# Mixture-of-experts tiles: singles between the pairs, weights used in place, programs written out

## The reference

```python
# layer 0: 8 experts, hidden 1024, two of them for a token, relu
h = relu(einsum('tc,efc->tef', x, w1) + b1);  y = einsum('tef,ecf->tec', h, w2) + b2
# layer 1: 8 experts, hidden 512, two of them for a token, gated
g = silu(einsum('bsd,edh->bseh', x, w1)) * einsum('bsd,edh->bseh', x, w2)
expert_out = einsum('bseh,ehd->bsed', g, w3)
# both: the token's two rows, weighted by the router's shares, are summed
```

## Time and profile before

| | us |
|---|---|
| median of 3 runs | 1726.03 |
| lowest, highest | 1717.77, 1727.92 |
| profiled execution, in all | 1718.13 |
| its span in the profile | 1716.4 |
| TensorE busy in the span | 1490.5 (87%) |
| VectorE, ScalarE, POOL busy | 1071.8, 818.4, 698.3 |

### The profile page before, as it was taken

The page is one execution under the profiler, slowest core; times in us unless marked ns, Lnnn a source line. Parts: engine busy times, 40 slices in busy tenths (PEclk is TensorE's granted clock), DMA queues, the critical chain, the costliest instruction groups (busy, mean ns, idle before and its releaser), DMA issues. The chain is left out here.

```text
span 1716.4 us, 37753 instructions
## 1 busy us (share of the span) xinstructions
PE 1490.5 (87%) x12752; PEld 1102.5 (64%) x12752; DVE 1071.8 (62%) x1904; ACT 818.4 (48%) x1552; POOL 698.3 (41%) x495
## 2 busy tenths in 40 slices
PE   7798898897888569999999887999978589999976
PEld 2433333334227558888888775777758479999875
DVE  5687687687787834555554333888868834444433
ACT  2664755665644425555555441666745322222221
POOL 3501402204200015666665432777750046666543
PEclk8899899899895689999999997999995789999999
DMA  5411321313116465555555664100007163344475
GB/s 180 147 50 49 122 73 58 113 49 117 63 43 221 147 238 131 143 144 138 144 139 115 190 183 109 46 25 25 26 6 241 62 209 63 63 65 66 105 215 137
DMA packets 110598, 191.45 MB, mean 112 GB/s; under 512 B 10929, under 2 KB 68581, under 8 KB 110181
## 3 DMA queue, kind: packets, MB, share of 16 engines
q1 hardware_dynamic: 80407, 149.44, 26.2%
q0 software_dynamic: 27264, 37.24, 12.6%
q10 hardware_dynamic: 2791, 2.84, 0.5%
HBM read 122.53 MB, written 66.96 MB: 110 GB/s over the span
## 5 line engine op out<-in xcount | busy, mean ns | idle before, releaser
L1391 PE MATMUL e_ph<-e_zTt,weights_a 128*128 128x256 f16 x2688 | 306.1, 275 | 2.3 <-DMA weights_b<-weight_parts 1.8
L1391 PEld LDWEIGHTS e_ph<-e_zTt,weights_a 128*128 x2688 | 262.5, 98 | 40.2 <-issue 8.4
L1321 POOL DMA_INDIRECT e_zt<-token_parts,slot_token x142 | 153.1, 1078 | 208.8 <-issue 199.2
L1474 ACT ACTIVATE e_h<-e_ph,e_b 128x256 f32<-128x256 f32 (+1 forms) x344 | 128.0, 434 | 208.6 <-PE e_ph L1391 146.6
L1529 DVE TENSOR_TENSOR e_hl<-e_h,e_hh 128x512 f16<-128x512 f32 x142 | 94.3, 690 | 202.8 <-ACT e_hh L1489 202.8
L1332 POOL DMA_INDIRECT token_rows<-e_ysb,slot_token x71 | 147.0, 2071 | 175.1 <-DVE e_ysb L1558 156.6
L1407 PE MATMUL e_pyt<-weights_b,e_hh 128*128 x1136 | 194.5, 274 | 4.3 <-issue 3.1
L704 ACT ACTIVATE probs<-lower_banks,shift 128x1024 f32<-128x1024 f32 x128 | 137.3, 1112 | 90.3 <-PE lower_banks L578 88.7
L1332 POOL DMA_INDIRECT out_dram<-e_ysb,slot_token x71 | 113.0, 1591 | 126.3 <-DVE e_ysb L1562 103.0
L1407 PE MATMUL e_pyt<-weights_b,e_hl 128*128 x568 | 155.5, 274 | 0.0
L739 DVE TENSOR_TENSOR acc<-acc,probs 128x1024 f32<-128x1024 f32 (+1 forms) x112 | 136.8, 1222 | 23.2 <-ACT probs L704 19.9
(11 more groups left out here) (251 smaller groups left out, 3000.0 us busy)
## 6 DMA issues: line engine op xcount, KB each, us to landing
x_sb<-weight_parts SPq DMA_DIRECT2D x30, 1024.0 KB, 7.1
weight_parts<-w_split SPq DMA_DIRECT2D x32, 512.0 KB, 3.4
weights_a<-weight_parts SPq DMA_DIRECT2D x16, 1024.0 KB, 7.4
x_sb<-in_u SPq DMA_DIRECT2D x24, 512.0 KB, 5.0
weight_parts<-x_sb SPq DMA_DIRECT2D x24, 512.0 KB, 3.4
w_raw<-in_w1T SPq DMA_DIRECT2D x16, 512.0 KB, 4.5
w_raw<-in_w2T SPq DMA_DIRECT2D x16, 512.0 KB, 4.8
weights_b<-weight_parts SPq DMA_DIRECT2D x8, 1024.0 KB, 9.3
```

The lines of the kernel that those rows point to most:

```text
L1321: pool.indirect_dma_start(zt[:, i % 2, c, :], None, g.zrows, at).then_inc(ld[i % 2], 16)
L1391: last = pe.matmul(out[:, f, :], up_of(i, e, wp, k, per * q + f), zTs[:, s, 2 * zp + k, 0:cols * P], start=(n == 0), stop=(n == 5))
L1474: last = act.activation(place(h32[:, slot], per)[:, f, :], place(ph[:, bank], per)[:, f, :], ACT.Relu, bias=b1[:, bass.ds(e, 1), per * q + ...
```

## The change

The tiles come in another order: 14 pairs, then single, pair, single, ..., the 43rd a single again (`SINGLES_FROM` = 13; `single[i]` and lists beside it take the place of `extent`). `column[i]` and `expert_of` map a tile to its old place in the tables, so routing stays as it is. `fetch_own`, its buffer and its semaphores go: a single's up takes the weights in `weights_a` by register address as a pair's does. A single's units use PSUM banks 0 to 1 (layer 0) or 0 and 2 (layer 1) and bank 1 of the downs. The programs of ScalarE and VectorE are written out for every tile, with constant semaphore values. In layer 0 VectorE copies the tokens of i+2 before the last of tile i+1's subtractions instead of behind it. TensorE reads the expert numbers in the middle of a pair's down only, so two at each pair among the singles.

```diff
+SINGLES_FROM = 2 * PAIRS - NT
...
+    single = [i > SINGLES_FROM and (i - SINGLES_FROM) % 2 == 1 for i in range(NT)]
+    cols = [1 if one else C for one in single]
+    per = [4 if one else 2 for one in single]
...
-            def fetch_own(i):
-
-                s, b = i % 2, i + PAIRS
-                if i >= PAIRS + 2:
-                    sp.wait_ge(up_done, UB * b - UB)
-                e = expert_of(sp, i)
-                sp.dma_start(own_w[:, s], g.parts[layer][:, :, bass.ds(e, 1), 0:2 * F0].rearrange("p w o n -> p w (o n)")
-                             ).then_inc(own_ld[s], 16)
...
-                if single:
-                    pe.wait_ge(own_ld[s], 16 * ((i - PAIRS) // 2 + 1))
                 pe.wait_ge(zev, i + 1)
...
-                                last = pe.matmul(out[:, f, :], up_of(i, e, wp, k, per * q + f), zTs[:, s, 2 * zp + k, 0:cols * P],
-                                                 start=(n == 0), stop=(n == 5))
+                                last = pe.matmul(out[:, f, :], up_w(wp, e, k, per[i] * q + f),
+                                                 zTs[:, s, 2 * zp + k, 0:cols[i] * P], start=(n == 0), stop=(n == 5))
...
-                for c in range(extent(i)[1]):
-                    if c == extent(i)[1] - 1 and i + 2 < NT:
-                        e[i + 2] = expert_of(pe, i + 2)
+                for c in range(cols[i]):
+                    if c == 1:
+                        for n in range(i + 2, min(i + 4, NT)):
+                            if n not in e:
+                                e[n] = expert_of(pe, n)
                     down(i, c, e[i])
...
+            for i in range(NT):
+                e = expert_of(act, i) if layer == 0 else None
+                activate(i, 0, e)
+                for q in units(i)[1:]:
+                    activate(i, q, e)
+                    high(i, q - 1)
+                high(i, units(i)[-1])
+                if layer == 0 and 0 <= i - FIRST_PIECE < PIECES:
+                    weight_high(i - FIRST_PIECE)
...
+            for i in range(-1, NT):
                 if i + 1 < NT:
-                    hidden_and_next(i + 1, (i + 1) % 2, i + 2 < NT, False, i + 1 >= PAIRS, i + 2 >= PAIRS)
-                result(i, i % 2, i // 2, False, i >= PAIRS)
+                    if layer:
+                        for q in units(i + 1):
+                            gated(i + 1, q)
+                    else:
+                        for q in units(i + 1)[:-1]:
+                            low(i + 1, q)
+                    if 2 <= i + 2 < NT:
+                        evacuate(i + 2)
+                    for q in units(i + 1) if layer else units(i + 1)[-1:]:
+                        low(i + 1, q)
+                if i >= 0:
+                    result(i)
```

More of the change, by code:

```diff
@@ L1253, in experts, with units, hidden, parted @@
         up_w, down_w = g.up_w, g.down_w
[L1255 to L1268, removed]
-        def expert_of(eng, i):
-            return eng.value_load(g.expert[0:1, bass.ds(i, 1)], min_val=0, max_val=E - 1)
+        def expert_of(eng, i):
+            n = PAIRS + alone[i] if single[i] else i - alone[i]
+            return eng.value_load(g.expert[0:1, n:n + 1], min_val=0, max_val=E - 1)
+        def units(i):
+            return range(2 * cols[i]) if layer == 0 else range(cols[i])
+        def hidden(x, q):
+            return x[:, q % 2]
+        def parted(x, i):
+            return x.rearrange("p (f t) -> p f t", f=per[i])
+        def finished(i):
+            return blocks[i - 1] if i >= 1 else 0
         @block.sync
         def _(sp):
+            def fetch(j):
+                fetched = g.pieces[1][j % KINDS][0](j // KINDS)
+                sp.dma_start(raw[:, j % 2:j % 2 + 1, :].rearrange("p o (k n) -> p (o k) n", k=fetched.shape[1]), fetched
+                             ).then_inc(w_ld[j % 2], 16)
             if layer == 0:
@@ L1429, in _ @@
                               start=True, stop=True)
-        def steps(eng, body):
-            body(0, 0, True)
-            body(1, 1, True)
-            for first, last in ((1, SPLIT), (SPLIT, PAIRS // 2)):
-                with eng.Fori(first, last) as n:
-                    body(2 * n, 0, False)
-                    if layer == 0 and first == 1:
-                        weight_high(eng, n, 0)
-                    body(2 * n + 1, 1, False)
-                    if layer == 0 and first == 1:
-                        weight_high(eng, n, 1)
-            for i in range(PAIRS, NT):
-                body(i, i % 2, False, True)
@@ new lines, in low @@
+            def low(i, q):
+                n = len(units(i)) // cols[i] * blocks[i] + q
+                if q == 0 and finished(i):
+                    dve.wait_ge(dn_done, finished(i))
+                dve.wait_ge(hi_done, n + 1)
+                own = (slice(None), i % 2, slice(per[i] * q, per[i] * q + per[i]), slice(0, cols[i] * P))
+                dve.tensor_tensor(hl[own], parted(hidden(gt if layer else h32, n), i), hh[own], ALU.subtract
+                                  ).then_inc(lo_done, 1)
@@ L1546, in result @@
+            def result(i):
+                if layer == 0:
+                    if i == 0:
                         dve.wait_ge(w_kept[1], 16)
                     e = expert_of(dve, i)
-                if not early:
-                    dve.wait_ge(sto[s], landed(i) if single else 16 * C * half)
-                for c in range(cols):
-                    share = g.slot_weight[:, bass.ds(b + c, 1)]
-                    y = py[s if single else c]
+                if i >= 2:
+                    dve.wait_ge(sto[i % 2], landed[i - 2])
+                for c in range(cols[i]):
+                    share = g.slot_weight[:, column[i] + c:column[i] + c + 1]
+                    y = py[out_of(i, c)]
+                    dve.wait_ge(dn_done, blocks[i] + c + 1)
@@ L1579, in _ @@
[L1579 to L1589 removed]
+            evacuate(0)
```

250 lines of the change are left out of this document (89 added, 161 removed).

## The result

The changed kernel takes **1769.0 us** (median of 4 runs, 1764.1 to 1773.8) against 1723.4 us (1717.8 to 1727.9) for the kernel before, run on the same chip: a ratio of 1.0265, 95% interval 1.0233 to 1.0297. It is slower by 45.7 us; the forecast was 1762 us, in a range from 1732 to 1784. The profiled execution took 1768.9 us with a span of 1767.2.

The account below looks back on a forecast made before the run. TensorE was taken as nearly full, its layer-0 pair matmuls nearly equal to the ScalarE/VectorE chain. Terms 34.5 - 1.2 + 5.4 + 1.7 gave +40 us, 1758 or 1766 by base; predicted 1762 us, range 1732 to 1784.

Parts of the forecast that it names:

- Layer 0, pair to single, 10.1 us: From a pair's up to the single's: the token copy behind the pair's third subtraction sets 10.1 us, against 8.1 of matmuls.
- Layer 0, single to pair, 10.1 us: From a single's up to the next pair's: 4.1 of register steps, 0.45, 5.24 and 0.3 of expert loads.
- Layer 1, 6.8 and 7.8 us: Pair to single 6.8 us, single to pair 7.8 along the sequencer; stretch 211.5 against 206.1 us, +5.4.
- The first pairs, 0.1 us each from the earlier copy, -1.2 us: Layer 0's first 13 pairs gain 0.1 us each from the earlier copy, since matmuls then bound them.
- Fetches' cost given back whole: Fetches' waits and slowed gathers, within 1.8 us a layer-1 single, at most 27 us in all, are won back whole.
- The statement that a reordering can win little: TensorE is 95% and 92% busy in the two stretches, so reordering wins little unless TensorE works on too much.
- Scatters: Scatters and gathers stay off the path in both layers; phase ends cost 0.6 us in layer 0, 1.1 in layer 1.
- Rival 4: Much slower: scatters set the pace, 15.6 us against layer 1's 14.6 us turn; 1776 to 1788 us, chance 0.10.
- Writing out, 0 within 0 to 5 us: Written-out ScalarE and VectorE programs mean more instruction fetching: bounded by 0 and +5 us, taken as 0.
- Rival 1: Faster: register steps of a single's up are hidden, layer 1's stretch 182 us; total 1707 us, chance 0.12.
- Rival 3: No difference: steps cost but layer 0's chain doesn't, stretch 265 us; total 1732 us, chance 0.08.
- The sequencer's lead: How far TensorE's register steps run ahead: at most 18 matmuls by the row, 0.2 to 0.3 us at layer-1 singles' ups.

Follow-up runs that it names:

- warm: The changed kernel with 24 unused transposes of the identity ahead of the wait for the copy at each layer-0 single; 1755.6 us, one run.
- fixed: The changed kernel, but every single's up reads expert 0's weights at a fixed address instead of the chosen expert's by register; 1712.8 us.
- loads_early: The changed kernel with TensorE's two loads of expert numbers moved from the pair's down into the middle of its up; 1752.0 us.
- late_copy: The changed kernel with layer 0's copy of turned tokens back behind a tile's last subtraction; 1770.0 us, 2 runs.
- tail_fetch: The changed kernel with the old tile order (pairs, then singles) and the singles' weight fetches put back; 1720.0 us.
- three_regs: The changed kernel with three buffers instead of two for layer 0's hidden tile; 1733.4 us.
- tail_regs: The changed kernel with the old tile order in both layers, still with register addresses and no fetches; 1727.7 us.

## Why the prediction was right, step by step

- **Layer 0, pair to single, 10.1 us**: 9.99. The mechanism is shown from both sides: a third buffer makes it 8.14, a later copy 10.59.
- **Layer 0, single to pair, 10.1 us**: 10.44 to 10.54 but for the first. The sum held at the full clock (10.04 in `warm`); what failed is that it took the clock of before for granted across a new gap. The fall to 1.2 GHz stretches the up from 4.2 to 4.8 us; it also gives the sequencer time, so that the loads' gap of 0.3 us, which the sum had, is covered. With the clock held the stretch is 293.8 us against 295.4 forecast.
- **Layer 1, 6.8 and 7.8 us**: 6.77 and 7.8 to 8.1, 214.3 us against 211.5. Steps and loads are both shown, by `fixed` (5.9) and `loads_early` (7.2).
- **The first pairs, 0.1 us each from the earlier copy, -1.2 us**: right in sign, but mostly not by that cause. `late_copy` has the copy in its old place and still 10.93 us a pair; the copy gave 0.6 us of 2.3, other edits the rest.
- **Fetches' cost given back whole**: right in sign, small in size. Alternating, fetching costs 3.1 us in layer 1 and 0.5 in layer 0. What hurt before was fetches and gathers crowded into a stretch of singles (12.4 us of waits in `tail_fetch`). The statement that a reordering can win little was wrong for layer 1: it wins 17.4 us when nothing else is changed.
- **Scatters**: no wait of TensorE for them or for gathers. POOL waited for its own scatters twice in layer 0's stretch (2.2 and 5.2 us) and never in layer 1's; TensorE shows no wait behind it. The end cost 0.6 us where 1.1 had been put for layer 1. Rival 4 falls.
- **Writing out, 0 within 0 to 5 us**: `tail_fetch` at 0.9987 bears it out.
- **Rival 1** (steps hidden, 1707 us) is what `fixed` built: 1712.8 us, its layer 1 at 189 instead of 182. Rival 3 (the chain doesn't cost) was 1732, with a stretch of 265 us; `three_regs`, which took the chain away, came to 1733.4, with 270.
- **The sequencer's lead**: in layer 0 a single's steps ran from 861.5 to 865.5 beside matmuls from 861.6 to 866.3. The first step stands behind the wait for the copy, so there the row says nothing of how far ahead the sequencer could get. In layer 1, where TensorE did not wait, they ran from 1612.6 to 1616.6 beside matmuls from 1612.7 to 1616.7, a lead of 0.1 us where 0.2 to 0.3 had been put. The Trainium skill, in Advanced Engine Details and Errata, section Engine Queue Depths, gives TensorE's queue as 64 deep. The longest lead that was measured here is the 18 matmuls of the row of before.

How near the total came is in part luck. In the profiled executions the changed code costs 42.4 us (50.8 less the 8.4 of the start), where the sum had 40.4. Layer 0's stretch came out 4.2 us above its term, mostly by the clock, layer 1's 2.8 above; the first 14 tiles lie 1.7 below theirs, and the ends with what lies between the layers 3.3 below. The medians differ by 45.7 us, but how the runs that were not profiled started is not known, so nothing finer than this can be read from them.

## What to carry to other kernels

A weight address from a register cost TensorE's sequencer about 0.13 us here (32 in 4.0 us); the 48 matmuls of 256 columns (5.24 us) cover them, 48 of 128 columns (2.7 us) don't, so small tiles are the wrong ones to use "in place". Before reordering tiles, write out for each the interval from its first up to the next tile's, by TensorE, by its sequencer and by the chain through the other engines: the longest of the three counts at each step, and an order can be right in one layer and wrong in the other. Test the parts of a combined change as a square, since here, in layer 1, one part won 17 us and the other took 22; and with one buffer less, ask what its refill stands behind in the queue of the engine that issues it.

## What the runs showed of the hardware

- A wait of 1.75 us followed by 48 matmuls thinned by register steps took TensorE from 2.4 to 1.2 GHz within the up (granted clock 0.65 over it, 0.92 over the stretch). With dense matmuls (`fixed`) 13 waits of 1.66 us did nothing and one of 1.93 us cost 1.3 us; thin matmuls without a wait (`tail_regs`), with two of 0.5 us (`three_regs`), or with it filled down to 0.41 us (`warm`), stayed at 1.00. A longer wait, 2.35 us ahead of thin matmuls, cost less (`late_copy`, 0.94 over the stretch).
- The first 36 us of the same instructions had a granted clock of 0.68 to 0.72 in five profiled executions and 0.93 to 0.97 in nine, worth 5.5 to 10.6 us at the start of layer 0. What decides it I don't know.
- Two loads of expert numbers in TensorE's program cost 0.8 us a turn in the middle of a pair's down (single to pair 8.0 us) and nothing in the middle of its up (7.2 us).
